# Hyperbolic half-steps at three of four positions, and zero products ahead of the scores' bank waits, in a two-layer attention kernel

## What is computed

```python
# plain heads (cosine heads: the same on normalised q and k)
scores = einsum('bhtd,bhsd->bhts', q, k) * scale + causal
out = einsum('bhts,bhsd->bhtd', softmax(scores), v)

# hyperbolic heads
tq = sqrt(1/curv + sum(q*q)); tk = sqrt(1/curv + sum(k*k))
inner = q @ k.T - tq * tk.T
arg = maximum(-curv * inner, 1 + 1e-07)
dis = sqrt(1/curv) * arccosh(arg)
scores = 1 / (1e-06 + dis) + causal
out = softmax(scores) @ v
```

## The kernel before, in words

| engine | at its position p |
|---|---|
| PE (`attention`, L779 to L790) | `scores(p+1)` in two pairs of heads, `values(p)`, `hyp_values` of the half-step of p-4, the remaining side jobs, `hyp_scores` of the half-step of p |
| ACT (L1036 to L1047) | two exps of the standard step p (L1029), then for the half-steps of p-4, p-3, p-2, p-1: exp (L1018), score (L1012 and L1013), log (L1007), root (L1001 and L1002) |
| DVE (L1370 to L1383) | output copies that are due (L1333), `hyp_arg` of the half-step of p-1 (L1343 reads PSUM, L1348 squares), half of the side jobs, `hyp_shift` of p-3 (L1356), the other side jobs |
| POOL (L1655 to L1670) | the masks of p and p-4 (L1572, L1580), two `lin` operations of p-2 (L1666), the sum of p-1 (L1670) |

## Time and profile before

### The profile page before, as it was taken

One profiled execution on the slowest core, in us unless ns is written; L12 is line 12 of the kernel. 1 busy time (PEld: TensorE's weight loads), 2 busy tenths in 40 slices (PEclk: granted clock), 3 DMA queues, 4 the chain that ended last, 5 costly groups with the idle time before them and its releaser, 6 DMA issues. The chain is left out here.

```text
span 2582.2 us, 30828 instructions
## 1 busy us (share of the span) xinstructions
PE 2217.8 (86%) x11109; PEld 873.0 (34%) x11109; DVE 1486.7 (58%) x3043; ACT 1343.8 (52%) x1923; POOL 833.9 (32%) x909
## 2 busy tenths in 40 slices
PE   6799976779999998778999999777899999877789
PEld 2233432234433342223443344222343334322243
DVE  6562556856556266675656445677565635577552
ACT  2345447962244635795225553688423454378922
POOL 1112125533411313562331221365142122146534
PEclk7899977879999986588999998767899999766889
DMA  5200231004310023100520022110051002401013
GB/s 145 67 15 18 67 99 36 1 1 119 101 28 2 21 78 83 36 1 13 143 72 20 2 66 80 36 36 1 23 156 42 20 2 83 98 9 27 1 53 88
DMA packets 67850, 128.38 MB, mean 50 GB/s; under 512 B 11397, under 2 KB 24837, under 8 KB 63077
## 3 DMA queue, kind: packets, MB, share of 16 engines
q1 hardware_dynamic: 67696, 126.40, 17.9%
HBM read 109.99 MB, written 15.20 MB: 48 GB/s over the span
## 5 line engine op out<-in xcount | busy, mean ns | idle before, releaser
L1281 DVE TENSOR_REDUCE mx<-ps 128x1 f32<-128x512 f32 (+3 forms) x992 | 612.5, 655 | 373.8 <-PE ps L620 241.3
L1029 ACT ACTIVATE pr<-ps 128x1024 f32<-128x1024 f32 (+3 forms) x672 | 515.0, 804 | 404.3 <-PE ps L690 403.7
L690 PE MATMUL ps<-qop,kop 75*128 75x512 bf16 (+7 forms) x1344 | 407.6, 367 | 123.1 <-DVE wb L1343 41.5
L617 PE MATMUL ps<-kop,qop 72*128 72x512 bf16 (+6 forms) x1248 | 425.4, 374 | 92.1 <-DVE mx L1281 69.7
L1572 POOL TENSOR_SCALAR_AFFINE_SELECT pr<-pr 128x512 f32<-128x512 f32 x224 | 145.5, 649 | 730.9 <-ACT pr L1029 730.1
L736 PE MATMUL ps<-pr,vt 128*32 128x512 f32 (+3 forms) x2688 | 340.4, 584 | 8.2 <-POOL pr L1572 7.6
L1090 ACT ACTIVATE pr<-ps 128x512 f32<-128x512 f32 x224 | 133.8, 597 | 337.6 <-PE ps L846 273.7
L617 PEld LDWEIGHTS ps<-kop,qop 72*128 72x128 bf16 (+1 forms) x1248 | 128.1, 105 | 424.9 <-DVE mx L1281 256.1
L690 PEld LDWEIGHTS ps<-qop,kop 75*128 75x128 bf16 (+1 forms) x1344 | 121.6, 104 | 361.7 <-ACT pr L1029 117.9
L856 PE MATMUL ps<-pr,w_down 128*128 128x512 f32 x384 | 196.7, 599 | 4.1 <-POOL pr L1563 4.1
L843 PE MATMUL ps<-hT,w_gate 128*128 128x512 f32 x384 | 196.2, 592 | 0.2 <-DVE on L1508 0.2
(11 more groups left out here) (316 smaller groups left out, 3153.0 us busy)
## 6 DMA issues: line engine op xcount, KB each, us to landing
wb<-gates_scratch SPq DMA_DIRECT2D x192, 256.0 KB, 3.4
kop<-kparts_scratch SPq DMA_DIRECT2D x32, 576.0 KB
qop<-qparts_scratch SPq DMA_DIRECT2D x96, 192.0 KB
on<-hmax_scratch SPq DMA_DIRECT2D x8, 1024.0 KB, 5.7
kparts_scratch<-on SPq DMA_DIRECT2D x12, 256.0 KB, 2.9
qparts_scratch<-on SPq DMA_DIRECT2D x12, 256.0 KB, 4.9
qparts_scratch<-wb SPq DMA_DIRECT2D x12, 192.0 KB
kparts_scratch<-wb SPq DMA_DIRECT2D x12, 192.0 KB
```

The lines of the kernel that those rows point to most:

```text
L617: mm = pe.matmul(o, qop[0:k, slot(l, u), j, qb * P:(qb + 1) * P], kop[0:k, slot(l, u), j, k0:k0 + wd], start=True, stop=not diag)
L690: mm = pe.matmul(o, kop[0:k, slot(l, u), 2 * pair + j, kb * P:(kb + 1) * P], qop[0:k, slot(l, u), 2 * pair + j, q0:q0 + wd], start=True, s ...
L1029: nc.scalar.activation(pr[:, g % 3, 2 * pair:2 * pair + 2, o0:o0 + wd], ps[:, bank:bank + 2, o0:o0 + wd], ACT.Exp).then_inc(a.exps, 1)
L1281: ins_ = nc.vector.tensor_reduce(mx[:, nth(l, u) % 2, j0:j0 + heads, qb, col % 2], ps[:, bank, 0:heads * wd].rearrange("p (j n) -> p j n", ...
```

## The change

Half-step k now enters at position 1 + k + k // 3: at 1, 2, 3, 5, 6, 7, 9 and so on up to 31, with 4, 8, 12, ... left free. Everything that hangs on the position of a half-step moves along on all engines; the side jobs keep theirs, except that the turns of hyperbolic outputs move with the outputs: the first hyperbolic output (c = 0) is copied at position 15 instead of 13, the second at 36 instead of 29, where the last standard one is copied too. The number of positions (37) stays.

In layer 1 PE issues `FILL` = 2 products of zero weights with 512 columns each before every `take_banks`, provided that an accumulation is open in bank 4 (standard) or, failing that, in bank 5 (hyperbolic): they add zero to it.

```diff
 HYP_UNIT = 3
+FILL = 2
...
 HYP_HALVES = 2 * NS
-HYP_POS = [1 + k for k in range(HYP_HALVES)]
+HYP_POS = [1 + k + k // 3 for k in range(HYP_HALVES)]
...
+                def add_zeros(bank, times):
+
+                    for _ in range(times):
+                        pe.matmul(ps[:, bank, :], zeros, identb[:].unsqueeze(1).broadcast_to([P, 4, P]),
+                                  start=False, stop=False)
+
+                def open_bank(std_done, hyp_done):
+
+                    if 0 < std_done <= STD_UNITS[l] * NS:
+                        c, kb = STEPS[(std_done - 1) % NS][:2]
+                        if kb != 4 * c + 3:
+                            return 4
+                    if 0 < hyp_done:
+                        c, kb = STEPS[(hyp_done - 1) // 2][:2]
+                        if hyp_done % 2 == 0 and kb != 4 * c + 3:
+                            return 5
+                    return None
+
+                def keep_busy(times):
+
+                    bank = open_bank(*values_done)
+                    if l and bank is not None:
+                        add_zeros(bank, times)
+
+                values_done = [0, 0]
                 score_job = [0]
...
                     for pair in range(2):
+                        keep_busy(FILL)
                         bank = take_banks()
...
                         pe.wait_ge(a.ops[HYP_UNIT], OPS_HYP)
+                    keep_busy(FILL)
                     bank = take_banks()
...
                         values(p, extra)
+                        values_done[0] = p + 1
                     if l and hyp_at(p - 4) != NOBODY:
                         hyp_values(hyp_at(p - 4))
+                        values_done[1] = hyp_at(p - 4) + 1
```

## The result

The changed kernel takes **2611.6 us** (median of four runs, 2603.9 to 2626.6) against 2563.0 (four runs too, 2552.5 to 2564.5): 1.0207 of the time before, 95% interval 1.0177 to 1.0236, so about 2% slower. I had forecast 2549 with a range of 2510 to 2586.

What follows compares the result with a forecast made beforehand. It took the DVE and PE chain to bound positions 0 to 11 and ACT's idle time to be what counts. Per stage -8.2 + 3.6 + 1.1 = -3.5, -14 us for four, off 2563.6: 2549, range 2510 to 2586.

Steps and rivals of the forecast that it cites:

- late stretch: Positions 12 to 35: moved ACT work added, idle falls from 13.5 to 9.4 us; +3.6 a stage, bounds 0 and +10.
- my 7.7: ACT work leaving positions 0 to 11 of a stage and coming back later: 7.7 us.
- roots behind arguments: New ACT waits of roots behind DVE's argument and square at positions 12, 15 and 19: 0.3 to 0.8 us.
- about 2 more: Positions 14 and 15: DVE has 6.7 us of work a position against ACT's 5; about 2 us more waiting.
- early stretch: Positions 0 to 11: shorter DVE and PE chain, less ACT work, faster clock; -8.2 us a stage, bounds -13 and +5.
- The stop: Ahead of step 12: ACT waits for the DMA of unit 1's maxima rows, so of the work that left only 2.3 us count.
- the clock and zero products: PE at positions 0 to 11: three blocks at full clock save 3.9 us, zero products cost 2.6; net -1.3 a stage.
- the 0.9 that I had named: Sign that the forecast is right: granted clock of the four stages above 0.9.
- slow rival: Zero products at half clock on PE's path at positions 1 to 10: +9.8 us a stage, 2603 in total; chance 0.18.
- Hidden anyway: Early stretch shortens by only 5.6 us, 5 come back late: +0.5 a stage with the end, 2566; chance 0.22.
- Regimes mix better: Late idle falls to 1.5 us, so positions 12 to 35 take 121.7: -11.4 a stage, 2518; chance 0.18.
- The end: Position 36: two outputs end together, one more copy of 0.69 plus mask and product; +1.1 us a stage, 0.5 to 2.

Runs made afterwards that it cites:

- p16: Changed kernel without zero products, unit 2's pieces of the maxima at positions 16 to 21 instead of 13 to 21: 2638.2 us, 1.0299 of before.
- s1: Changed kernel with FILL = 0, so the new half-step positions without zero products: 2619.1 us, 1.0221 of before.
- s2: Changed kernel with the old half-step positions, so zero products alone: 2568.3 us, 1.0021 of before.
- s3: Kernel before, no zero products, first 15 half-steps kept at 1 to 15, other nine at three of four positions up to 27: 2563.0 us, 1.0003.
- swn: Changed kernel without zero products, unit 1's maxima rows sent ahead of the hyperbolic unit's second spread: 2621.7 us, 1.0199 of before.
- swo: Kernel before, unit 1's maxima rows sent ahead of the hyperbolic unit's second spread: 2557.5 us, 0.9968 of before.

## Why the prediction was wrong

**The step that failed is the late stretch: "Idle 9.4; 129.6 against 126.0: +3.6".** I cut at step 12 and took all of 12 to 35 as bound by ACT. The work across that cut was right (7.0 us against my 7.7). But positions 12 to 15 lost 9.1 us of ACT's work (28.27 to 19.14 in the first stage) and got no shorter: a chain of PE and DVE holds them at some 29 us. Unit 2's pieces are 4.4 of it (p16); for the rest ACT's waits name the half-steps' arguments (7.9 us), which no run takes away. I had priced this as 0.3 to 0.8 for roots behind arguments and "about 2 more" at 14 and 15. Measured: 11.0 us idle (30.1 less 19.1) there, and 19.9 in the whole stretch, past my bound of 15.8. Behind step 16 ACT does bound the stage, as I had it: s1 brings 16.1 us of work there and is 16.9 longer. The earlier trace rows misled me: with 112.5 of 126.0 us busy ACT looked like the only limit, and at 12 to 15, where it had almost no idle time, that hid a second chain as long.

**The early stretch** was the second miss: -8.2 forecast, -3.5 measured (the mean of four stages, 83.9 to 80.5). The DVE work that goes at 4 to 7 (26.6 to 24.9 us in s1) brought nothing there (35.2 to 35.8), where the pieces are the floor. The stop came as named, and cost more than I said: it swallowed 5.5 us. The 2.3 us that I let the stretch gain ahead of it were too many: I counted the first pair of scores as 0.4 us, but in s1 ACT's exps began 1.07 us behind the scores (434.32 to 435.39), which leaves about 1.7. Of the clock and zero products I had -1.3 net, and the difference of s1 and the changed kernel over 0 to 11 is -1.4 (81.8 to 80.5).

**Zero products** were judged right: they lift the clock (in s2, with the old order, to 0.83 at positions 0 to 11 and 0.92 at 12 to 35 of the first stage; 0.71 and 0.75 before), though the changed kernel's stages came to 0.86 to 0.88 and not above the 0.9 that I had named, and they are not the loss. My slow rival gave 2603, close to the time, by a mechanism that s1 and s2 exclude: the one place where the rows above show zero products at half clock on the path is step 12, 1.7 us by the starts. In the changed kernel's trace they save 14 us over four stages (888.7 to 874.8); by the ratios of s1 and the changed kernel, 1.0221 and 1.0207, this is within the noise. (The Trainium skill, Perfetto Trace Analysis, section Identifying the Most-Contended Engine, has one judge TensorE's headroom by its weight-load time; in s2's positions 24 to 35 this is 54.2 of 153.9 us, and the products cost 4.2 us a stage there all the same.)

**"Hidden anyway"** had the mechanism, "early ACT time was free, late ACT time is not", with the size wrong: I let 5 us come back late, and positions 12 to 35 got 13.6 longer (124.7 to 138.3, means of four stages); its sign, an early stretch over 77 us, came (80.2). "Regimes mix better" is refuted: late idle time is 19.9 us, where its sign was under 4, and s3, which mixes the late positions alone, stays at 1.0003. (By the Trainium skill, Perfetto Trace Analysis, section Optimization Strategy, interleaving regimes may help; no run here that spreads the half-steps gains by it.)

**The end** was right: two copies stand back to back,

```profile
576.49 1.29 DVE L1363 COPY osb<-ps 128x512 f32<-128x512 f32 x2 [1.27 <-PE ps L764]
```

1.29 us against 0.69. That every half-step keeps ACT's total, 678 us, was right too; which stretch holds it decides.

## What to carry to other kernels

Work that fills one engine's time in a stretch where another chain is as long should not be moved into a stretch bound by that engine: here it gave back a quarter (4.3 of 16.2 us a stage) and cost nearly in full (14.4). Before pricing such a move, cut the stretch finer than its phases and ask of each piece what it would take with the work gone; little idle time is no proof that no other chain is waiting behind. Filler for the clock belongs where its engine waits, not where it sets the pace; even so, filler alone won nothing here that can be told from noise.

## What was not expected of the hardware

A small transfer's landing was set by the large one ahead of it on SP's queue. PE went on at step 12 6.54 to 6.58 us after the issue of the 1 MB spread in three kernels (before, changed, s1), though the rows were issued 1.54 us behind it before and 0.43 in the other two; in the changed kernel the zero products begin then, the scores 0.83 us later. The page of the changed kernel has the spread itself landing after

```profile
on<-hmax_scratch SPq DMA_DIRECT2D x8, 1024.0 KB, 5.8
```

and the rows sent first landed after 3.2 us (430.52 to 433.72 in swn, 425.01 to 428.21 in swo). (The Trainium skill, DMA: Bandwidth & Descriptors, section Queues, rings and completion order, says that each DMA engine takes descriptors in ring order; the trace agrees.) And in s2 a clock of 0.83 and 0.92 in place of 0.71 and 0.75, got with zero products, bought nothing in the total (1.0021): by the table a stage got 4.5 us shorter ahead of position 24 and 4.4 longer behind it.
